# Two copies of the payload and slot buffers, used in turn by the groups of a routed attention and expert kernel

## The chip, the cores and the metric

The kernel runs on one core of a Trainium2 chip. The metric is the device time of the launch in microseconds, as the median of several runs. TensorE (PE), VectorE (DVE), ScalarE (ACT), GpSimd (POOL) and SyncE (SP) each run their own queue of instructions and meet at semaphores. DMAs are issued by SP, ACT and POOL and carried out by 16 DMA engines.

## What is computed

The input `x` is 16 x 128 x 256 (2048 tokens of width 256). First comes a gated convolutional attention, then a layer norm and a routed mixture of experts, both added to `x` (cut from the reference):

```python
kv = jnp.einsum('bhil,bhjl->bijhl', k_, v_)                     # k = v = ctx
y = irfft(rfft(kv, n=512) * rfft(ssm_kernel, n=512))[..., :256] # causal convolution
out = jnp.einsum('bijhl,bhil->bjhl', y + kv * D, q_)            # q = layernorm(x)
x = x + tanh(g_xattn) * out
# experts: E=32 of width 176, the best 6 by score, from 4 of 8 groups, and a shared one
scores = sigmoid(xf @ w_router); sfc = scores + corr_bias       # xf = layernorm(x)
topk_idx = top_k(where(group_mask, sfc, -inf), 6)
routed = sum over the 6 of scores[e] * (silu(xf @ gate_w[e]) * (xf @ up_w[e])) @ down_w[e]
shared = silu(xf @ sh_gate_w) * (xf @ sh_up_w) @ sh_down_w
x = x + tanh(g_ffn) * (routed + shared)
```

## The kernel before

The work has three stages.

**Stage one: the groups.** The 16 batch rows are taken in NG = 4 groups of GB = 4, so 512 tokens in each. A step `group(g, attend, route)` exists on each compute engine. It routes group g and, beside it, does the attention of group g + 1; the first step (g = -1) only attends, the last one (g = 3) only routes. The order within a step is written out by hand on each engine:

- VectorE: products of the context for the next group (L574), then the attention's result is added to `rows` (L715), a layer norm (L551 to L565, which ends by raising `norm_done`), the first half of the product with q and the sum of pairs of the next group (`times_q(0)`, L590, and `sum_pairs(0)`, L603), then `choose()` (from L620: it picks six experts per token) and `place_rows` (L695 to L704: it writes the place of each token in its experts' lists into `slots`), and then the second half of the next group. In group 3 there is no next group, so `choose()` follows the norm at once.
- ScalarE: normalizes and copies; before the rows of group g are written into `payload` (L448) it waits at L444 for `norm_done` and at L445 for `payload_free`.
- TensorE: attention transposes (L909), convolution (L898, L899), transposes of `payload` (L921), router (L965), shared expert (L930, L940, L949).
- POOL: for each group it waits for `slots_ready`, then issues 24 indirect DMAs (L358), each of which scatters 128 rows of 289 floats (256 of the row, the token's number, 32 scores) from `payload` to the experts' lists in HBM, waits until all 24 have landed (L361) and raises `payload_free` (L362). It is raised once before the groups.
- SP: for each group it stores four tiles of the shared expert's result to HBM (`store_shared`, L255 to L261), one after another: each is waited for before the next is issued. ScalarE's copy of a tile to be stored (L419) waits for its buffer, one of two.

**The expert weights** fill one SBUF arena, `w_gu` (32 experts, one row of each of the 128 partitions for all) and `w_down` behind it (88 partitions). The same arena holds what the groups work on, so only a part of the weights can be loaded early: experts 0 to EARLY - 1 of `w_gu` (L253, by SP at the start). The rest of `w_gu` and the first WD_MID experts of `w_down` are loaded by ScalarE in the last group, right behind the writing of `payload` (L454 to L457); the next ones up to WD_LAST by ScalarE when the tables are ready (L483), the last ones by SP behind its last store (L267).

**Stage two: the loop over expert tiles.** SP waits for the tables and for `payload_free` of all groups (L283, L284), reads some values from a table, and loads the first tiles of 128 rows from the lists to `payload` (L274). TensorE waits for all weights and then does, per tile, transposes (L1018), gate and up (L1027), transposes (L1037) and down (L1046). POOL adds each result to the tokens' sums in HBM (L372). There are 108 tiles.

**Stage three**: the sums are loaded, added to `rows` (L871 to L875) and stored.

Of the kernel before, what the change touches and what calls it, by code (L numbers as in the profile page):

```python
# [5 lines left out]
P = 128  # L6
B, HD, L = 16, 128, 256
NH, DH = 16, 8
BLK = L // P
GB = 4  # L10
# [15 lines left out]
TOK_AT, SCORE_AT = L, L + 1  # L26
EARLY = 15
EPS = 1e-5
# [18 lines left out]
WIDE_AT = TMP_AT + TMP_SIZE - 3 * P  # L47
X2T_AT = TMP_AT + TMP_SIZE
SILU_AT = X2T_AT + GB * L
# [32 lines left out]
def build(nc, x, ctx_t, toeplitz, g_xattn, g_ffn, skip_d, w_router, corr_bias,  # L82
# [10 lines left out]
    with ctx:  # L93
# [34 lines left out]
        earlier = sb("earlier", [P, NGRP, NGRP])  # L128
        slots = sb("slots", [P, GB, DH], u32)
        norm_x = sb("norm_x", [P, 2, B])  # L130
# [12 lines left out]
        ctx_v = win(arena, CTX_AT, [[BLK * HD * GB, NG], [HD * GB, BLK], [DH * GB, NH], [1, DH * GB]])  # L143
        toe_v = win(arena, TOE_AT, [[L, NH], [1, L]])
        router_sb = win(arena, ROUTER_AT, [[E, KC], [1, E]])
        stats = win(arena, STATS_AT, [[6, B], [1, 6]])
# [82 lines left out]
        def _(sp):  # L229
# [35 lines left out]
            store_shared(NG - 1)  # L265

            sp.dma_start(wd[:, WD_LAST * WD_E:E * WD_E], w_down[:, WD_LAST * WD_E:E * WD_E]).then_inc(late_in, 16)  # L267

# [34 lines left out]
        def _(pool):  # L303
# [49 lines left out]
            for g in range(NG):  # L353
                pool.wait_ge(slots_ready, g + 1)
                pool.sem_inc(held, 1)
                for b in range(GB):
                    for k in range(TOPK):
                        nc.gpsimd.indirect_dma_start(  # L358
                            lists, bass.IndirectOffsetOnAxis(ap=slots[:, b, k:k + 1], axis=0),
                            payload[:, b, :], None).then_inc(scattered, 16)  # L360
                pool.wait_ge(scattered, (g + 1) * (GB * TOPK * 16))  # L361
                pool.sem_inc(payload_free, 1)  # L362
# [30 lines left out]
        def _(act):  # L393
# [4 lines left out]
            def group(g, attend, route):  # L398
# [43 lines left out]
                if route:  # L442

                    act.wait_ge(norm_done, g + 1)  # L444
                    act.wait_ge(payload_free, g + 1)  # L445
                    act.sem_inc(held, 1)
                    for b in range(GB):
                        last = nc.scalar.activation(payload[:, b, 0:L], rows[:, bass.ds(g * GB + b, 1), :],  # L448
                                                    ACT.Identity, bias=norm[:, 1, b:b + 1], scale=norm[:, 0, b:b + 1])
# [8 lines left out]
                    for p in range(2):  # L458
# [4 lines left out]
                    act.wait_ge(logits_ready, g + 1)  # L463
                    nc.scalar.activation(payload[:, :, SCORE_AT:ROW], win(bank[4], 0, [[E, GB], [1, E]]),
                                         ACT.Sigmoid).then_inc(scores_ready, 1)
# [11 lines left out]
            for g in range(NG - 1):  # L477
# [3 lines left out]

            act.wait_ge(tables_ready, 1)
            act.dma_start(wd[:, WD_MID * WD_E:WD_LAST * WD_E],  # L483
                          w_down[:, WD_MID * WD_E:WD_LAST * WD_E]).then_inc(late_in, 16)
# [47 lines left out]
        def _(dve):  # L532
            count = [0]

            def group(g, attend, route, start):
# [81 lines left out]
                def choose():  # L617

                    dve.wait_ge(scores_ready, g + 1)
                    nc.vector.tensor_copy(payload[:, :, TOK_AT], tok_id[:, bass.ds(g * GB, GB)])  # L620
                    at = [TMP_AT]
# [10 lines left out]

                    scores = payload[:, :, SCORE_AT:ROW]
                    sfc = tmp(GB, E)
# [55 lines left out]
                def place_rows(onehot, part, bke, tmp):  # L690
# [12 lines left out]
                                                 AX, ALU.add))  # L703
                    nc.vector.tensor_copy(slots[:, :, 0:TOPK], win(arena, slot_f, [[TOPK, GB], [1, TOPK]])).then_inc(slots_ready, 1)  # L704

# [174 lines left out]
        def _(pe):  # L880
# [6 lines left out]
            def group(g, attend, route):  # L887
# [71 lines left out]
                if route:  # L959
                    transpose_rows(lambda b, k: payload[:, b, k * P:(k + 1) * P],  # L960
                                   x2_ready, lambda p: g * 2 + p + 1, 0, x2T_ready)
# [155 lines left out]
```

## Time and profile before

| | |
|---|---|
| median of 3 runs | 627.01 us |
| lowest, highest | 623.39, 627.03 us |
| the profiled execution | 621.08 us (span of the instructions 619.0 us) |
| mean granted TensorE clock in it | 0.886 |
| busy in it: PE, DVE, ACT, POOL | 469.5, 331.4, 204.0, 281.4 us |

The rows come from the one profiled execution. Times are from the start of the span. An idle wait is put down to the instruction that ended it ("releaser"); `x24` is the number of instructions in a row of a view. A letter q behind an engine's name (ACTq, POOLq, SPq) marks its queue's own instructions: DMA issues, semaphores, register loads. The DMA queues are q0 (issued by POOL), q1 (by SP) and q10 (by ACT).

### The profile page before, as it was taken

How to read it: one execution, taken by the hardware profiler on the slowest of the kernel's cores; microseconds unless marked ns; L12 is line 12 of the kernel's file. 1: busy time of each engine (PE TensorE's matmuls, PEld its weight loads, DVE VectorE, ACT ScalarE, POOL GpSimd, SP SyncE). 2: the span in 40 equal slices, each digit the busy share in tenths (PEclk: the TensorE clock that was granted, in tenths of full speed). 3: DMA queues.
4: the chain of work that ended last, by engine and by line, in shares of the span. 5: the costliest groups of instructions: out<-in, count | busy, mean ns of one | idle time of the engine just before them, and what ended most of it. 6: DMA issues, size and time to landing. Idle time of an engine off the chain costs nothing.

```text
span 619.0 us, 8968 instructions
## 1 busy us (share of the span) xinstructions
PE 469.5 (76%) x2271; PEld 358.6 (58%) x2271; DVE 331.4 (54%) x1169; ACT 204.0 (33%) x510; POOL 281.4 (45%) x243
## 2 busy tenths in 40 slices
PE   0365889959968981692069999999999999999900
PEld 0355766846756671471047777777777777777600
DVE  3798689578866931660024444444444444444327
ACT  2140632443335312220014444444444444444400
POOL 3600006711770374067106666666666666666620
PEclk9996989959996996686569999999999999999955
DMA  7999103300330134977636666666666666666478
GB/s 266 346 342 434 56 1 112 125 29 16 134 116 0 53 136 176 356 183 221 164 79 108 115 111 115 112 116 118 110 110 114 119 111 113 111 116 120 64 232 337
DMA packets 55756, 89.70 MB, mean 145 GB/s; under 512 B 6573, under 2 KB 49933, under 8 KB 55053
## 3 DMA queue, kind: packets, MB, share of 16 engines
q0 software_dynamic: 20160, 28.37, 26.5%
q1 hardware_dynamic: 35198, 49.87, 24.3%
q10 hardware_dynamic: 342, 10.81, 5.7%
q8 instruction: 24, 0.39, 0.3%
q14 instruction: 32, 0.25, 0.1%
HBM read 47.00 MB, written 42.03 MB: 144 GB/s over the span
## 4 chain that ended last, share of the span: by engine, by line
PE 51%; POOL 13%; DMA 13%; DVE 13%; issue 6%; ACT 2%; SPq 1%; POOLq 0%; DVEq 0%; ACTq 0%
PE bank L1027 21%; PE bank L1046 15%; POOL expert_lists L358 12%; DMA token_sums<-arena 6%; PE bank L1018 4%; PE bank L1037 4%; DVE arena L590 3%; DMA arena<-token_sums 2%; DMA arena<-toeplitz 2%; PE bank L965 2%; DVE work L603 2%; PE bank L909 2%; PE bank L921 1%; DMA expert_lists<-payload,slots 1%; PE bank L898 1%
## 5 line engine op out<-in xcount | busy, mean ns | idle before, releaser
L372 POOL DMA_INDIRECT token_sums<-work,dest x108 | 168.3, 1558 | 127.1 <-ACT work L505 103.5
L358 POOL DMA_INDIRECT expert_lists<-payload,slots x96 | 98.8, 1029 | 172.3 <-DVE slots L704 144.2
L1027 PE MATMUL bank<-wgu,work 128*128 x432 | 148.1, 466 | 0.1
L1046 PE MATMUL bank<-wd,work 88*128 x432 | 111.0, 379 | 0.0
L849 DVE TENSOR_TENSOR work<-work,bank 128x176 f32<-128x176 f32 x108 | 36.4, 337 | 121.7 <-ACT work L490 121.7
L1027 PEld LDWEIGHTS bank<-wgu,work 128*128 128x128 f32 x432 | 74.5, 192 | 24.0 <-issue 1.5
L831 DVE COPY work<-bank 128x256 f32<-128x256 f32 x108 | 45.8, 424 | 60.0 <-PE bank L1018 60.0
L1046 PEld LDWEIGHTS bank<-wd,work 88*128 88x128 f32 x432 | 73.3, 190 | 6.1 <-issue 0.2
L490 ACT ACTIVATE work<-bank 128x176 f32<-128x176 f32 x108 | 34.2, 317 | 126.6 <-PE bank L1027 126.6
L505 ACT ACTIVATE work<-bank,work 128x256 f32<-128x256 f32 x108 | 51.1, 473 | 53.6 <-DVE work L843 52.3
L1018 PE MATMUL bank<-ident,payload 128*128 128x128 f32 x216 | 42.1, 276 | 23.5 <-DMA payload<-expert_lists 23.5
L1018 PEld LDWEIGHTS bank<-ident,payload 128*128 128x128 f32 x216 | 30.8, 144 | 35.4 <-DMA payload<-expert_lists 24.2
L930 PE MATMUL bank<-shgu_sb,arena 128*128 128x352 f32 x128 | 51.3, 554 | 0.0
L590 DVE TENSOR_TENSOR arena<-arena,q_sb 128x448 f32<-128x448 f32 (+7 forms) x120 | 43.2, 434 | 7.9 <-ACT arena L405 7.8
L898 PE MATMUL bank<-arena 128*128 128x288 f32 x128 | 43.9, 426 | 1.2 <-ACT arena L405 1.2
L1037 PEld LDWEIGHTS bank<-ident,work 128*88 128x88 f32 x216 | 26.6, 123 | 30.3 <-issue 19.0
L1037 PE MATMUL bank<-ident,work 128*88 128x128 f32 x216 | 41.3, 273 | 0.0
L949 PE MATMUL bank<-shd_sb,arena 88*128 88x256 f32 x128 | 32.9, 402 | 11.1 <-ACT arena L414 10.1
L909 PE MATMUL bank<-ident,work 128*128 128x128 f32 x256 | 31.3, 286 | 12.9 <-DVE work L603 12.9
L497 ACT COPY work<-bank 88x256 f32<-88x256 f32 x108 | 39.7, 367 | 0.0
L909 PEld LDWEIGHTS bank<-ident,work 128*128 128x128 f32 x256 | 31.2, 203 | 13.2 <-issue 13.1
L930 PEld LDWEIGHTS bank<-shgu_sb,arena 128*128 128x128 f32 x128 | 28.5, 234 | 14.3 <-issue 7.2
(140 smaller groups left out, 512.1 us busy)
## 6 DMA issues: line engine op xcount, KB each, us to landing
payload<-expert_lists SPq DMA_DIRECT2D x108, 144.5 KB, 2.6
arena<-token_sums SPq DMA_DIRECT2D x12, 512.0 KB, 8.3
wgu<-w_gu ACTq DMA_DIRECT2D x1, 5984.0 KB
wgu<-w_gu SPq DMA_DIRECT2D x1, 5280.0 KB, 31.3
expert_lists<-blank SPq DMA_DIRECT2D x1, 4768.5 KB, 24.2
token_sums<-blank SPq DMA_DIRECT2D x1, 4480.0 KB, 34.3
wd<-w_down ACTq DMA_DIRECT2D x1, 3520.0 KB
arena<-toeplitz SPq DMA_DIRECT2D x1, 2048.0 KB, 11.3
```

What stands on the lines that cost most here:

```text
L358: nc.gpsimd.indirect_dma_start(lists, bass.IndirectOffsetOnAxis(ap=slots[:, b, k:k + 1], axis=0), payload[:, b, :], None).then_inc(scatter ...
L372: nc.gpsimd.indirect_dma_start(sums, bass.IndirectOffsetOnAxis(ap=dest[:, t % NPICK:t % NPICK + 1], axis=0), y_row(t), None, compute_op=AL ...
L505: nc.scalar.activation(y_row(t), bank[6 + t % 2][:, 0:L], ACT.Identity, scale=pick_w(t)).then_inc(t_y_copied, 1)
L590: last = nc.vector.tensor_tensor(win(arena, Z_AT + z0, [[DH * DH * GB, HB], [(DH + 1) * GB, DH - d], [1, GB]]), y, win(q_sb, s * HB * DH * ...
L831: nc.vector.tensor_copy(win(work, XT_AT + t % 2 * L, [[1, L]]), bank[t % 2][:, 0:L]).then_inc(t_x, 1)
L898: nc.tensor.matmul(y[:, 0:2 * CB], toe(h, 0), prods(s, hh, 0, 2), start=True, stop=False)
L909: last = nc.tensor.matmul(bank[p][:, (b * BLK + k) * P:(b * BLK + k + 1) * P], win(work, ((k * 4 + i) * GB + 2 * p + b) * P, [[1, P]]), id ...
L930: last = nc.tensor.matmul(bank[5 + half][:, 0:SHM], x2T(b, k), shgu_sb[:, k, half * SHM:(half + 1) * SHM], start=(k == 0), stop=(k == KC - 1))
L1018: last = nc.tensor.transpose(bank[t % 2][:, k * P:(k + 1) * P], payload[:, t % NX, k * P:(k + 1) * P], ident[:, :])
L1027: last = nc.tensor.matmul(bank[2 + t % 2][:, 0:2 * M], xT_half(t, k), wgu[:, bass.ds(e * WGU_E + k * 2 * M, 2 * M)], start=(k == 0), stop= ...
L1037: last = nc.tensor.transpose(bank[4 + t % 2][0:MH, c * P:(c + 1) * P], win(work, H_AT + t % 2 * M + c * MH, [[1, MH]]), ident[:, :])
L1046: last = nc.tensor.matmul(bank[6 + t % 2][:, 0:L], hT_half(t, c), wd[:, bass.ds(e * WD_E + c * L, L)], start=(c == 0), stop=(c == 1))
```

## The change

Two copies of `payload` are used in turn: groups 0 and 2 write a new one, `pay[0]`, which lies in the arena, groups 1 and 3 the old one. `slots` gets a second copy as well. ScalarE waits before it writes group g's rows for the scatters of group g - 2, no longer for those of group g - 1. Since the arena has to hold 1156 floats per partition more, what lies in front of it moves down by two experts' `w_gu`: EARLY is 13 for 15, so 19 experts of `w_gu` are loaded late for 17 (6688 KB for 5984), with WD_MID = 17 and WD_LAST = 25 for 20 and 26. The first late part of `w_down` is so 17 experts for 20, the second 8 for 6, the last 7 for 6. The second and the last part would overwrite `pay[0]`, so they wait for group 2's scatters.

```diff
-EARLY = 15
+EARLY = 13
...
-X2T_AT = TMP_AT + TMP_SIZE
+PAY_AT = TMP_AT + TMP_SIZE
+X2T_AT = PAY_AT + GB * ROW
...
-        slots = sb("slots", [P, GB, DH], u32)
+        slots = sb("slots", [P, 2, GB, DH], u32)
...
+        pay = [win(arena, PAY_AT, [[ROW, GB], [1, ROW]]), payload[:, :, :]]
...
+            sp.wait_ge(payload_free, NG)
             sp.dma_start(wd[:, WD_LAST * WD_E:E * WD_E], w_down[:, WD_LAST * WD_E:E * WD_E]).then_inc(late_in, 16)
...
-                            lists, bass.IndirectOffsetOnAxis(ap=slots[:, b, k:k + 1], axis=0),
-                            payload[:, b, :], None).then_inc(scattered, 16)
+                            lists, bass.IndirectOffsetOnAxis(ap=slots[:, g % 2, b, k:k + 1], axis=0),
+                            pay[g % 2][:, b, :], None).then_inc(scattered, 16)
...
-                    act.wait_ge(payload_free, g + 1)
+                    act.wait_ge(payload_free, max(1, g))
                     act.sem_inc(held, 1)
                     for b in range(GB):
-                        last = nc.scalar.activation(payload[:, b, 0:L], rows[:, bass.ds(g * GB + b, 1), :],
+                        last = nc.scalar.activation(pay[g % 2][:, b, 0:L], rows[:, bass.ds(g * GB + b, 1), :],
...
-                    nc.scalar.activation(payload[:, :, SCORE_AT:ROW], win(bank[4], 0, [[E, GB], [1, E]]),
+                    nc.scalar.activation(pay[g % 2][:, :, SCORE_AT:ROW], win(bank[4], 0, [[E, GB], [1, E]]),
...
             act.wait_ge(tables_ready, 1)
+            act.wait_ge(payload_free, NG)
             act.dma_start(wd[:, WD_MID * WD_E:WD_LAST * WD_E],
...
-                    nc.vector.tensor_copy(payload[:, :, TOK_AT], tok_id[:, bass.ds(g * GB, GB)])
+                    nc.vector.tensor_copy(pay[g % 2][:, :, TOK_AT], tok_id[:, bass.ds(g * GB, GB)])
...
-                    scores = payload[:, :, SCORE_AT:ROW]
+                    scores = pay[g % 2][:, :, SCORE_AT:ROW]
...
-                    nc.vector.tensor_copy(slots[:, :, 0:TOPK], win(arena, slot_f, [[TOPK, GB], [1, TOPK]])).then_inc(slots_ready, 1)
+                    nc.vector.tensor_copy(slots[:, g % 2, :, 0:TOPK], win(arena, slot_f, [[TOPK, GB], [1, TOPK]])).then_inc(slots_ready, 1)
...
-                    transpose_rows(lambda b, k: payload[:, b, k * P:(k + 1) * P],
+                    transpose_rows(lambda b, k: pay[g % 2][:, b, k * P:(k + 1) * P],
```

## Rows read from the trace of the kernel before

**Rows 1.** The page's chain that ended last, by line, as shares of the span.
```profile
PE bank L1027 21%; PE bank L1046 15%; POOL expert_lists L358 12%; DMA token_sums<-arena 6%; PE bank L1018 4%; PE bank L1037 4%; DVE arena L590 3%; DMA arena<-token_sums 2%; DMA arena<-toeplitz 2%; PE bank L965 2%; DVE work L603 2%; PE bank L909 2%; PE bank L921 1%; DMA expert_lists<-payload,slots 1%; PE bank L898 1%
```

**Rows 2.** By stretch: busy us of PE, PEld, DVE, ACT, POOL; clock, DMA share, GB/s.
```profile
350.00:588.00 238.00, 236.93 (x1142) 175.52 (x1140) 107.55 (x470) 101.92 (x288) 149.61 (x97) 1.00 0.66 111
```

**Rows 3.** Waits: who waited for whom, us in total, times, longest us.
```profile
ACT payload L448 <- POOLq L362: 30.9, 3, 19.5
```

**Rows 4.** Timeline of DVE, groups 1 and 2: start, us, instructions, [idle before, releaser].
```profile
129.15 3.77 DVE L603 TENSOR_TENSOR work<-arena 128x256 f32<-128x256 f32 x8
137.25 0.17 DVE L620 COPY payload<-tok_id 128x4 f32<-128x4 f32 x1 [4.33 <-ACT payload L464]
...
186.22 3.77 DVE L603 TENSOR_TENSOR work<-arena 128x256 f32<-128x256 f32 x8
194.54 0.17 DVE L620 COPY payload<-tok_id 128x4 f32<-128x4 f32 x1 [4.56 <-ACT payload L464]
```

**Rows 5.** Timelines of DVE and ACT in group 3.
```profile
235.37 0.16 DVE L565 SCALAR_TENSOR_TENSOR norm<-arena,norm 128x4 f32<-128x4 f32 x1
...
242.90 0.60 ACT L448 ACTIVATE payload<-rows,norm 128x256 f32<-128x256 f32 x1 [19.45 <-POOLq L362]
243.01 0.38 ACTq L455 DMA_DIRECT2D wgu<-w_gu  x1
...
250.79 0.17 DVE L620 COPY payload<-tok_id 128x4 f32<-128x4 f32 x1 [15.26 <-ACT payload L464]
```

**Rows 6.** POOL: last scatter of group 2, first and last of group 3; L362's first and last.
```profile
240.00 0.96 POOL L358 DMA_INDIRECT expert_lists<-payload,slots  x1 [0.30 <-issue]
265.99 0.96 POOL L358 DMA_INDIRECT expert_lists<-payload,slots  x1 [25.03 <-DVE slots L704]
...
295.14 0.96 POOL L358 DMA_INDIRECT expert_lists<-payload,slots  x1 [0.30 <-issue]
...
L362 POOLq EVENT_SEMAPHORE  x4: 17/17/17, 129.2 to 302.4; - x4
```

**Rows 7.** DMA queues (packets, MB, share) in 209-243, 244-259, 260-265, 270-275, 265-280, 283-284 us.
```profile
q0 software_dynamic: 1152, 3.55, 28.9%
...
q10 hardware_dynamic: 142, 6.33, 103.6%
...
q10 hardware_dynamic: 20, 0.82, 79.8%
...
q1 hardware_dynamic: 45, 0.04, 2.3%
...
q10 hardware_dynamic: 47, 1.93, 56.9%
q0 software_dynamic: 176, 0.56, 11.3%
q1 hardware_dynamic: 61, 0.06, 1.4%
...
q10 hardware_dynamic: 8, 0.00, 0.7%
```

**Rows 8.** Chain that ended last, in order of time: start, us, what.
```profile
269.14 16.85 DMA token_sums<-arena
...
286.07 6.24 DMA token_sums<-arena
...
292.38 9.54 DMA token_sums<-arena
...
303.80 0.34 SPq L267
...
305.51 7.86 DMA payload<-expert_lists
...
314.21 1.19 PE bank L1018 x4
```

**Rows 9.** The page's DMA issues: tiles, queue, count, KB each, median us to landing.
```profile
payload<-expert_lists SPq DMA_DIRECT2D x108, 144.5 KB, 2.6
```

## The prediction

> **What bounds the kernel now.** I read the page's chain by line first [rows 1]: 44% of the span is TensorE in the loop over expert tiles (L1027, L1046, L1018, L1037), and 12% is POOL at L358, the scatters of routed rows. The table by stretches [rows 2] shows that loop full: from 350 to 588 us TensorE is busy 236.93 of 238 us at full clock. The change leaves that loop and the tail alone (108 tiles, same instructions), so what it is worth is how much earlier the loop's first transpose (314.21 us, [rows 8]) comes.
>
> In the first part the wait to look for is ScalarE's at L448, for the queue of POOL at L362 [rows 3]: 30.9 us in three waits, the longest 19.5. A group may not write `payload` before the scatters of the group before have landed. TensorE and VectorE stand behind it.
>
> After the last group two lines of work run to the loop's start [rows 6, 8]. One is POOL: 24 scatters from 265.99, the last issued at 295.14, all landed at 302.4 [rows 6]. The other is SP: four stores of the shared expert's rows, one after another (16.85, 6.24, 9.54 us and a short one), then the last part of `w_down` at 303.80 and the first tile's load at 305.51. They end 1.4 us apart. Both are slow for one reason, the late expert weights issued at 243.01.
>
> **The change, part by part.**
>
> *Group 1.* Its L448 starts at 129.28, when payload comes free, 5.58 us late. VectorE gives part of that back: it sums pairs from 129.15 for 3.77 us (to 132.92) and only then starts to choose experts, at 137.25 [rows 4]. Without the wait the scores, which let 137.25 go, come 5.6 us earlier (131.6), before 132.92. So choosing starts at 132.95: 4.3 us gained, not 5.6.
>
> *Group 2.* The same: 186.22 + 3.77 = 189.99, against 194.54 [rows 4]: 4.5 us. Together 8.8.
>
> *Group 3.* There is no next group's attention to do. The norm's last step is issued at 235.37 for 0.16 us and L448 starts at 242.90 [rows 5]. Allowing 0.2 us it would start at 235.7: 7.2 us. Nothing else of VectorE's lies between, so this shows in full: choosing at 250.79 − 16.0 = 234.8, and slots for the last scatters 16.0 us earlier too; POOL could start them at 265.99 − 16.0 = 250.0.
>
> The new waits for scatters two groups back cost nothing here: group 2 needs those of group 0 (landed 129.2, [rows 6]) at some 176, group 3 those of group 1 (landed some 57 us later, a group's period, less 4) at 227. The copies' other address, and `slots` with one more dimension, add no instruction.
>
> *What comes next.* If everything followed, the loop would start 16 us earlier. But the wait also held back the late weights. ScalarE issues them right behind L448: 243.01 becomes 227.0, with the first bytes about 1 us later, at 227.9. POOL issues one scatter each 29.15/23 = 1.27 us, group 2's last at 240.00 [rows 6], after the change 231.2. It lands about 2.8 us from the start of its issue (240.00, and L448 goes on at 242.90). So the last five, issued from 226.1 on, have packets left when the weights begin. Before, all had landed first.
>
> What that costs is read from group 3's scatters, which run beside the weights' second part. One scatter is 1152/24 = 48 packets [rows 7], 3 per DMA engine. Of the weights' 142 packets from 244 to 259 us some 133 carry data (6.33 MB of 48 KB each, `w_gu`'s rows), which makes 1.036 × 15 us × 16/133 = 1.87 us for one on its engine; a `w_down` packet is 41 KB and took 0.798 × 5 × 16/20 = 3.2 us, before any scatter ran beside it [rows 7]. `w_gu`'s 128 rows are 8 packets per engine and are through at about 259.2. `w_down` has 88 rows. Of the first shared store's 144 packets (9 per engine) 45 went through in 270 to 275 us, at once, and only 16 more by 280: so 5 engines are free and 11 work on `w_down`, 8 packets each [rows 7, 8]. From 265 to 280 us 176 scatter packets went through; ten scatters had reached the free engines, 5 × 3 × 10 = 150; the other 26 passed on the 11 busy ones beside 47 weight packets, 0.55 small ones to a large one. The small packets wait behind large ones, and few pass.
>
> After the change five scatters leave 15 small packets per engine, with 8 + 8 = 16 large ones on the 11 busy engines. At 0.55 per large one some 9 pass before the weights end, and the shared store's went at a similar pace (16 packets on 11 engines in 5 us), so the scatters land when the weights end. The end: before, first bytes 243.9, `w_gu` to 259.2, the last data at 283.6 (from 283 to 284 its queue shows only packets without data, [rows 7]). After, 19 experts for 17 make `w_gu` 15.2 × 19/17 = 17.0 us, 17 for 20 make `w_down` 24.4 × 17/20 = 20.7 us, and the extra small packets cost 1.3 us (ten data packets of 0.2 us, less what the 24.4 hold already): 227.9 + 39.0 = 266.9. POOL waits for them before it may start group 3's, which I put 0.8 us later: **267.8**. Before it was 265.99. The 16 us that the groups give are gone for POOL.
>
> If instead one small packet passed for each large one, the 15th small one would be through before the last large one starts, 20.7/8 = 2.6 us before the weights' end: POOL starts at 265.0. The row's 0.55 is below that. The Trainium skill, "DMA: Bandwidth & Descriptors", section "Queues, rings and completion order", says that each DMA engine takes the queues in turn, a packet from each; by that rule the alternation is strict and the loop starts 13 us earlier, by the row 10.
>
> *From there to the loop.* Last scatter 29.15 us after the first (265.99 to 295.14), landing 2.75 us as group 2's last one did (group 3's own took 7.3, [rows 6], beside the second part of `w_down`, which now comes 20 us earlier), SP's value loads 1.4 us (303.80 to 305.51 less 0.34 of issue), the first load 2.6 us (the median, [rows 9]; here 7.86 behind the last part of `w_down`), and 0.1 to 0.84 us until TensorE starts (take 0.2): 267.8 + 29.15 + 2.75 + 1.4 + 2.6 + 0.2 = 303.9, against 314.21: **10.3 us**.
>
> *The stores, against it.* The first lands 2.4 us behind the weights' end (285.99 against 283.6, [rows 8]), 269.3; the second has no backlog of group 3's scatters beside it (some 2 us, not 6.24), 271.3; the third lies beside the second part of `w_down`, now 8 experts for 6: 9.54 × 8/6 = 12.7 at most, 284; the fourth 1.7; the last part of `w_down`, 7 for 6, some 8 to 10 us: 296. That is 8 us ahead of 303.9. The costs of the shift in weights (704 KB more late `w_gu`, 528 KB less late `w_down` of the first part) are in the sum above, the early load of 13 for 15 experts lies beside group 0's attention and nothing waits for it until the loop.
>
> **The rivals.**
>
> *Scatters pass freely.* If group 2's five scatters land in time for slots (250.0), POOL is done at 282, and the stores decide: first at 269.3, second 6.2 beside group 3's backlog, third 9.5 to 12.7, fourth 1.7, then 10.4 to 11.6 from the last part of `w_down` to TensorE: 298 to 302, 12 to 16 us gained. For it: the five free engines pass all. Against it: a DMA is done when all 16 are.
>
> *Strict alternation* (above, one small packet to a large one): POOL starts at 265.0, 13.1 us gained. Against it the 0.55; for it, that the 0.55 comes from a time with two small queues.
>
> *A longer stall.* The backlog of 15 packets per engine isn't drained when weights end, or the shared stores take turns too: each 1 us is 1 us. At 5 us more, 5 us gained.
>
> *Slower than before.* `w_gu` packets now share the engines with scatters. If that brought them to the `w_down` packets' rate (41 KB in 3.2 us, so 53.5 KB in 4.2), 8 of them take 33.6 us for 17: POOL starts at 284.4, 6 us slower than before. It decides from 3.4 us a packet, at which the 10.3 us are gone. Against it: `w_down` packets were that slow with no scatter about.
>
> *It doesn't do what it says*: L448 still waits for the old scatters. Nothing in the diff does that.
>
> **How the numbers follow.** The profiled execution took 621.08 us (span 619.0); less 10.3 it is 610.8. The median of the three runs is 627.01, 6 us above it, and 623.39 the lowest; I forecast against the median: 616.7. Chances: landing at the weights' end 0.50, strict alternation 0.17, scatters pass freely 0.15, a longer stall 0.12, slower 0.03, no effect 0.03. The range from 16 us gained (611), less 2 for a median as near to the profiled run as 623.39 is, to 5 gained (622): 609 to 622. About 1% (6.3 us) is what a measurement tells from no change. Faster by over 1%: 0.86; within: 0.10; slower: 0.04.
>
> **What would show it.** L448 no longer waits for L362; choosing starts at 133.0, 185.7 and 234.8; weights issued at 227; group 2's last scatter lands at 264 to 269 and POOL starts group 3's right behind it, at 268, some 18 us after its slots are ready; SP waits at L284 for payload_free from about 296; the loop starts at 304. I am wrong if POOL starts at 250, if ScalarE finds group 1's scatters not landed, or if the loop's start moves and the end doesn't.

## The result, and the profile after

| | before | after |
|---|---|---|
| median | 625.96 us of 4 runs (623.39 to 627.03) | 608.29 us of 4 runs (607.58 to 608.84) |
| ratio, 95% interval | | 0.972 (0.969 to 0.976) |
| the profiled execution | 621.08 us (span 619.0) | 607.58 us (span 605.5) |
| mean granted TensorE clock | 0.886 | 0.894 |
| first transpose of the loop | 314.21 us | 301.71 us |

The change gains 17.7 us in the medians and 13.5 us between the two profiled executions. The forecast was 616.7 us with 609 as its lower end, so it came out too slow by 8.4 us, and just outside its range. Line numbers from L358 on are three or four higher after the change (L448 is L451, L358 is L361, L620 is L624).

VectorE's timeline after the change, at the lines where choosing starts (start, us, what, in brackets the idle time before and its releaser). The tile named `arena` is the new copy of the payload.

```profile
131.89 0.17 DVE L624 COPY payload<-tok_id 128x4 f32<-128x4 f32 x1
...
186.15 0.17 DVE L624 COPY arena<-tok_id 128x4 f32<-128x4 f32 x1
...
236.64 0.17 DVE L624 COPY payload<-tok_id 128x4 f32<-128x4 f32 x1 [8.04 <-ACT payload L467]
...
250.83 0.18 DVE L708 CAST slots<-arena 128x24 uint32<-128x24 f32 x1
```

Before, these three stood at 137.25, 194.54 and 250.79 [rows 4, 5]. The groups give 14.15 us by the last one; 16.0 was forecast. ScalarE's timeline in the last group shows the wait for POOL gone and the late weights issued right behind the first row of the payload:

```profile
228.74 0.60 ACT L451 ACTIVATE payload<-rows,norm 128x256 f32<-128x256 f32 x1 [12.06 <-DVE norm L569]
228.85 0.38 ACTq L458 DMA_DIRECT2D wgu<-w_gu  x1
```

POOL's timeline: the last scatter of group 2, then the first and the last of group 3; the last line is POOL's signal that a group's scatters have landed, with its first and last start.

```profile
231.11 0.96 POOL L361 DMA_INDIRECT expert_lists<-arena,slots  x1 [0.30 <-issue]
252.21 0.95 POOL L361 DMA_INDIRECT expert_lists<-payload,slots  x1 [20.14 <-DMA expert_lists<-arena,slots]
...
281.26 0.96 POOL L361 DMA_INDIRECT expert_lists<-payload,slots  x1 [0.30 <-issue]
...
L365 POOLq EVENT_SEMAPHORE  x4: 17/17/17, 128.3 to 289.9; - x4
```

And the chain that ended last, in order of time (start, us, what). It runs through the four stores of the shared expert's rows, the last part of `w_down` and the first tile's load:

```profile
254.72 15.87 DMA token_sums<-arena
270.67 6.25 DMA token_sums<-arena
277.00 11.61 DMA token_sums<-arena
288.69 1.74 DMA token_sums<-arena
290.51 0.34 SPq L270
292.22 8.82 DMA payload<-expert_lists
301.71 0.70 PE bank L1022 x2
```

The last scatter of group 2 was issued at 231.11, its last packet left an engine at 250.4, and it landed at 251.3 (20.2 us after its issue), where 266.9 was forecast. That is 0.3 us behind the slots (250.83 + 0.18). Before, POOL started 1.00 us after the writing of the slots began (264.99 and 265.99), here 1.38 us after, so some 0.4 us of its wait is still for the scatters. The stores decided the loop's start, with POOL's last landing (289.9) 0.6 us ahead of them.

### The profile page after: what moved, and what is told of

Read it like the earlier page. It is cut to its first block, busy times and chain, and to the rows that moved or that the text cites. A ratio compares the mean times of both kernels' runs of the same rounds, so it can differ in the third digit from the quotient of the medians.

```text
span 605.5 us, 8969 instructions
## 1 busy us (share of the span) xinstructions
PE 468.5 (77%) x2271; PEld 358.6 (59%) x2271; DVE 330.8 (55%) x1169; ACT 203.6 (34%) x510; POOL 281.0 (46%) x243
## 4 chain that ended last, share of the span: by engine, by line
PE 62%; DVE 18%; DMA 12%; ACT 2%; issue 2%; POOL 2%; SPq 1%; DVEq 0%; POOLq 0%; ACTq 0%
PE bank L1031 21%; PE bank L1050 15%; DMA token_sums<-arena 6%; DVE arena L594 6%; PE bank L913 5%; PE bank L1022 4%; PE bank L1041 4%; PE bank L934 4%; PE bank L953 3%; DVE work L607 3%; PE bank L902 2%; DMA arena<-toeplitz 2%; DMA arena<-token_sums 2%; DMA payload<-expert_lists 1%; DMA token_sums<-work,dest 1%
## 5 line engine op out<-in xcount | busy, mean ns | idle before, releaser
L361 POOL DMA_INDIRECT expert_lists<-arena,slots x48 | 49.6, 1033 | 105.1 <-DVE slots L708 91.1
L361 POOL DMA_INDIRECT expert_lists<-payload,slots x48 | 48.9, 1020 | 54.6 <-DVE slots L708 20.4
L934 PE MATMUL bank<-shgu_sb,arena 128*128 128x352 f32 x128 | 52.8, 567 | 0.0
L902 PE MATMUL bank<-arena 128*128 128x288 f32 x128 | 43.9, 426 | 1.2 <-ACT arena L408 1.2
L953 PE MATMUL bank<-shd_sb,arena 88*128 88x256 f32 x128 | 32.6, 400 | 9.5 <-ACT arena L417 9.2
```

The lines of the kernel that those rows point to most:

```text
L361: nc.gpsimd.indirect_dma_start(lists, bass.IndirectOffsetOnAxis(ap=slots[:, g % 2, b, k:k + 1], axis=0), pay[g % 2][:, b, :], None).then_i ...
L902: nc.tensor.matmul(y[:, 0:2 * CB], toe(h, 0), prods(s, hh, 0, 2), start=True, stop=False)
L934: last = nc.tensor.matmul(bank[5 + half][:, 0:SHM], x2T(b, k), shgu_sb[:, k, half * SHM:(half + 1) * SHM], start=(k == 0), stop=(k == KC - 1))
L953: last = nc.tensor.matmul(bank[4][:, 0:L], win(arena, HST_AT + c * P, [[1, P]], parts=MH), shd_sb[:, c, :], start=(c == 0), stop=(c == 3))
```

## Experiments

The theory at this point: the last group's stores decide, and group 2's scatters pass the weights because few of them are left when the weights begin. Rivals: the layout itself (fewer early experts) gives or costs something; the wait in the last group matters, or only those in groups 1 and 2; the part of the gain that the traces don't show is chance. The runs were made on several chips. Each has its own runs of the kernel before beside it.

### Taking the change apart, on a chip where it brings nothing

The edits are against the changed kernel (one line replaces another, three variants shown together). The first keeps the layout and both copies but waits as the old kernel does; the second takes the gain in groups 1 and 2 alone; the third in group 3 alone; the fourth is the changed kernel unedited.

```diff
-                    act.wait_ge(payload_free, max(1, g))
+                    act.wait_ge(payload_free, g + 1)                                       # layout only
+                    act.wait_ge(payload_free, g + 1 if g == NG - 1 else max(1, g))         # groups 1 and 2
+                    act.wait_ge(payload_free, g if g == NG - 1 else g + 1)                 # group 3
```

> The changed kernel with ScalarE's old wait put back (for the scatters of the group before): two copies, EARLY 13 and the new split of the late weights stay. Theory (the gain is the wait, the layout is neutral): the loop starts within 2 us of before's 314.2, time within 2 us of before. Rival (part of the 13 us of the traces comes from the layout, since less w_down and more w_gu goes into the first late part): 3 us or more faster than before, loop start at 311 or earlier.

> The changed kernel, but in the last group ScalarE waits for group 2's scatters as before; groups 1 and 2 don't. Theory (the loop starts a fixed stretch after the late weights are issued, because the shared stores stand behind them): weights issued at about 234 (scatters of group 2 landed), 9 us earlier than before and 5 later than in the changed kernel; loop start at 306 to 307, 7 to 8 us faster than before. Rival (the five scatters beside the weights cost the changed kernel something): as fast as the changed kernel or faster.

> The changed kernel, but groups 1 and 2 wait as before and only the last group does not. Theory: choosing starts at 137 and 194.5 as before, the last group's L448 follows the norm at about 236, 7 us earlier than before, so the weights are issued 7 us earlier and the loop starts 5 to 7 us earlier; together with the run of groups 1 and 2 the gains add up to the whole. Rival (POOL, not the stores, decides): group 2's scatters land only when the weights end, POOL starts the last group's no earlier than before (266) and the gain is under 2 us.

> The changed kernel again, on the chip of the three others. Theory (its runs agree and those of the kernel before spread by some us, the profiled one of before being the lowest): 607 to 609 us in each run, the kernel before at 621 to 627. Rival (the chip of the first comparison was odd): the kernel before within 1 us of 621, gain of 13 us as in the traces.

Measured, against a before of 659.9 us (31 runs): layout only 1.002 (0.999 to 1.005), groups 1 and 2 1.006 (1.001 to 1.010), group 3 1.002 (0.998 to 1.006), the changed kernel 1.006 (1.002 to 1.010). On this chip the kernel before takes 34 us more than on the first and the changed one 55 us more, and the change was worth nothing; if anything it cost 0.6%. No theory expected this. Waits of the changed kernel on this chip (who waited for whom, us in total, times, longest us), and two gaps in the timeline of weight loads to TensorE:

```profile
PEld bank L902 <- issue: 14.1, 8, 3.6
PEld bank L953 <- issue: 12.3, 9, 4.9
...
121.98 0.30 PEld L902 LDWEIGHTS bank<-arena 128*128 128x128 f32 x2 [2.44 <-issue]
126.27 0.50 PEld L902 LDWEIGHTS bank<-arena 128*128 128x128 f32 x2 [3.44 <-issue]
```

TensorE's stream of instructions stands still for microseconds while scatters run, with nothing in the profile that it waits for. The same waits on the first chip are 0.4 us (L902) and 0.2 us (L953) in all. TensorE isn't alone: in the same trace VectorE stands for 2.82 us before L719 and ScalarE for 4.62 us before L408, also with no releaser. Choosing here starts at 80.19, 146.55 and 213.18 us: a group takes 66 us instead of 53 to 54. Scatters then have landed long before the next payload is written. In the layout-only kernel, which still waits for them, the wait is not there to remove; ScalarE's one long wait at that line is for the norm:

```profile
ACT payload L451 <- DVE norm L569: 25.6, 1, 25.6
```

So on a chip in this condition the wait for `payload_free` costs nothing, and taking it away gives nothing. Why the engines stand still there was not found.

### The stores taken away, on a second such chip

The last group's four tiles go to four places in `q_sb`, free by then, so that ScalarE needn't wait for a buffer nor SP for a store.

```diff
-            store_shared(NG - 1)
+            for b in range(GB):
+                sp.wait_ge(sh_copied, (NG - 1) * GB + b + 1)
+                sp.dma_start(sums[0:T, :]..., win(q_sb, b * L, [[L, 1], [1, L]])).then_inc(sh_stored, 16)
...
-                    act.wait_ge(shared_free, g * GB + b + 1)
+                    if attend:
+                        act.wait_ge(shared_free, g * GB + b + 1)
...
+                    nc.scalar.copy(... if attend else win(q_sb, b * L, [[1, L]]), bank[4][:, 0:L])...
```

> The changed kernel, and in the last group the four tiles of the shared expert's result go to four buffers (q_sb, which that group has no use for) and are stored without a wait between them; the last part of w_down then follows their issue. In a loop start decided by the stores (first store's 15.9 us, then 6.3, 11.6 and 1.7, last part of w_down at 290.5): stores issued by 262, second and last part of w_down issued by 263, loop start 5 to 10 us earlier than the changed kernel's 301.7, then bound by POOL's scatters (last issued at 281, landed by 285 to 290). Rival (POOL's scatters decide already): loop start within 2 us of the changed kernel's.

Measured: 657.69 against 656.08 us, ratio 1.001 (0.997 to 1.006). The chip was again one where TensorE stands still, so this says nothing of the stores on the others. It was run again below.

### The weights in small packets

The two late loads behind the payload are cut into eight, so that a packet is 8 to 14 KB for 52 (`w_gu`) and 34 (`w_down`). TensorE's wait for the weights counts the added loads (not in the excerpt).

```diff
-                        act.dma_start(wgu[:, EARLY * WGU_E:E * WGU_E], ...).then_inc(late_in, 16)
-                        act.dma_start(wd[:, 0:WD_MID * WD_E], ...).then_inc(late_in, 16)
+                        for i, j in ((13, 18), (18, 23), (23, 28), (28, 32)):
+                            act.dma_start(wgu[:, i * WGU_E:j * WGU_E], ...).then_inc(late_in, 16)
+                        for i, j in ((0, 5), (5, 9), (9, 13), (13, 17)):
+                            act.dma_start(wd[:, i * WD_E:j * WD_E], ...).then_inc(late_in, 16)
```

> The changed kernel with the two late loads that ScalarE issues in the last group cut into eight (w_gu in parts of 5, 5, 5 and 4 experts, w_down in 5, 4, 4 and 4), so that a packet is 8 to 14 KB and not 35 to 54. Theory (each DMA engine takes a packet from each queue in turn, so a small packet waits for one large one): group 2's scatters and the first shared store get through three to four times faster; the first store lands in 3 to 6 us, not 15.9, though the weights end at about the same time. Rival (the store waits for the bytes of the weights, whatever their packets): it still takes 13 us or more.

Measured: a single run of each, 605.2 us against 623.67 us for the kernel before, so this is no comparison of medians. POOL's start no longer waits for any DMA, but for its slots:

```profile
255.74 0.96 POOL L361 DMA_INDIRECT expert_lists<-payload,slots  x1 [22.14 <-DVE slots L709]
...
284.89 3.18 DMA expert_lists<-payload,slots
289.47 8.68 DMA payload<-expert_lists
```

The scatters passed the weights. POOL started 3.5 us later than in the changed kernel: the weights were issued 2.1 us later in this execution (230.94), and eight issues on ScalarE delayed the scores by some 2 us more. The first store took 9.9 us, between the 3 to 6 of the theory and the 13 of its rival: it landed when the weights ended, at 268. From the first store's issue to the last one's landing it was some 29 us, where the changed kernel took 35.7. SP then still had to wait 0.5 us for POOL. The loop started at 298.87, for 301.71.

### The parts again, on a chip that behaves as the first

> The changed kernel with ScalarE's old wait put back, again, on another chip, since on the first TensorE stood still for microseconds beside the scatters. Theory (the gain is the wait, the layout is neutral): the loop starts within 2 us of before's 314.2 and the time is within 3 us of before's. Rival (part of the gain is the layout): 4 us or more faster than before.

> The wait relaxed in groups 1 and 2 only, again, on another chip. Theory (the loop starts a fixed stretch, some 73 us, after the late weights are issued): weights issued at about 234 and loop start at 306 to 307, 7 to 9 us faster than before, 5 slower than the changed kernel. Rival (group 2's scatters beside the weights cost the changed kernel something): within 2 us of the changed kernel.

> The wait relaxed in the last group only, again, on another chip. Theory: weights issued at about 236, loop start at 307 to 309, 5 to 7 us faster than before. Rival (POOL decides and its last 24 scatters start no earlier than before's 266, as the prediction had it): under 2 us.

| kernel | median | against before (625.0, 19 runs) | weights issued | loop starts |
|---|---|---|---|---|
| layout only | 625.5 | 1.000 (0.998 to 1.001) | 246.82 | 319.35 |
| groups 1 and 2 | 613.44 | 0.983 (0.978 to 0.987) | 235.12 | 306.99 |
| group 3 | 621.74 | 0.995 (0.993 to 0.997) | 237.72 | 312.67 |

The layout costs nothing. Groups 1 and 2 are worth 12 us, more than the 8.8 that the forecast gave them, and group 3 alone is worth 3.8 us, less than the theory's 5 to 7. Why groups 1 and 2 give more than forecast shows on ScalarE (the waits for the old scatters), first in the profile of before:

```profile
129.28 2.08 ACT L448 ACTIVATE payload<-rows,norm 128x256 f32<-128x256 f32 x4 [5.58 <-POOLq L362]
186.57 2.08 ACT L448 ACTIVATE payload<-rows,norm 128x256 f32<-128x256 f32 x4 [5.87 <-POOLq L362]
```

In the layout-only kernel, with one scatter each of groups 0 and 1 on POOL:

```profile
130.87 2.08 ACT L451 ACTIVATE payload<-rows,norm 128x256 f32<-128x256 f32 x4 [6.80 <-POOLq L365]
190.36 2.08 ACT L451 ACTIVATE arena<-rows,norm 128x256 f32<-128x256 f32 x4 [8.05 <-POOLq L365]
...
108.52 3.59 POOL L361 DMA_INDIRECT expert_lists<-arena,slots  x1 [0.30 <-issue]
166.78 3.59 POOL L361 DMA_INDIRECT expert_lists<-payload,slots  x1 [0.30 <-issue]
```

Most scatters are issued in 0.96 us and some in 3.59; the profile of before has none above 1.58. In a kernel that waits for them, each such one delays the next group. The kernel with group 3 alone bears it out: it waits 5.32 us in group 1, with no long scatter ahead, and 7.99 us in group 2, with one (at 165.17). Less the 1.3 us that VectorE gives back in each group, 6.80 and 8.05 make 12.3 us, and the weights came 11.7 us earlier. That the two agree so well is partly chance: the two executions start to choose 1.2 us apart, and TensorE ran slow in one group of the one and in two of the other (see below). In the changed kernel nobody waits. That would fit the spread too, 623.39 to 627.03 us before and 607.58 to 608.84 after, but no trace of a slower run of before is there to show it.

Group 3 alone is the forecast's mechanism in full, and the rival of this run came true in it: POOL decided. Four scatters of group 2 were behind the weights. The chain, and POOL's timeline:

```profile
241.61 26.58 DMA expert_lists<-arena,slots
...
269.09 0.95 POOL L361 DMA_INDIRECT expert_lists<-payload,slots  x1 [26.53 <-DMA expert_lists<-arena,slots]
...
298.17 10.86 DMA expert_lists<-payload,slots
```

POOL started 31.4 us after the weights' issue and decided the loop's start. In the changed kernel it started 23.4 us after, with three scatters behind the weights. Queues over the stretch from the weights' first bytes to the landing (packets, MB, share of 16 engines), first of the changed kernel (229.8 to 251.5 us), then of group 3 alone (238.7 to 268.5):

```profile
q10 hardware_dynamic: 166, 7.61, 90.9%
q0 software_dynamic: 144, 0.44, 5.1%
```

```profile
q10 hardware_dynamic: 199, 8.76, 84.1%
q0 software_dynamic: 192, 0.59, 5.8%
q1 hardware_dynamic: 45, 0.04, 0.4%
```

144 packets are 3 scatters, 9 packets per engine; 192 are 4 scatters, 12 per engine. Of q10's, 128 are `w_gu`'s (53.5 KB each, with KB of 1000 bytes here, 6.85 MB) and the rest of the bytes make 22 `w_down` packets of 34.8 KB in the first case and 55 in the second, which on 11 engines is 2 and 5 each (16 more carry no data): 8 + 2 = 10 large ones beside 9 small ones, and 8 + 5 = 13 beside 12. That is one small packet to one large one, behind one large one of head start. The fourth scatter's three packets per engine wait for three packets of `w_down`, and these are what the 8 us between 23.4 and 31.4 pay for, an estimate of 2.7 us each.

### The stores taken away, again

The same edit as on the second chip.

> The changed kernel with the last group's four shared stores in buffers of their own and without waits between them, again, on another chip. Theory (in the changed kernel the stores decide the loop's start): all weights are issued by 264, the loop starts at 290 to 296, 6 to 11 us earlier than in the changed kernel, bound then by POOL's scatters. Rival (the weights' bytes decide in any order): within 3 us of the changed kernel.

Measured: 606.79 us, ratio 0.970 (0.966 to 0.974); the changed kernel in the first batch, on another chip, had 0.972. Expected was a loop start at 290 to 296, it came at 300.15, within 3 us of the changed kernel's, as the rival had it. The chain:

```profile
282.85 13.68 DMA expert_lists<-payload,slots
298.76 2.33 DMA payload<-expert_lists
```

POOL had started and ended its issues within 1.6 us of the changed kernel's. The landing took 13.68 us, 5 more than there, because without the stores' waits both remaining parts of `w_down` are issued at 268.0 and 268.72 and are moved beside the scatters. In the changed kernel the stores were last, but right behind them comes POOL. Whether the bytes of the weights would hold the loop up in any order, as the rival says, this run doesn't settle. Here too three scatters were issued late enough to be caught, and POOL started 23.5 us after the weights' issue.

### TensorE kept busy ahead of the shared expert

In the changed kernel TensorE idles 2.6 to 3.1 us for VectorE before the shared expert's products of each attending group. TensorE's timeline, and a table of 6 us (busy us and instructions of PE, PEld, DVE, ACT, POOL; granted clock, DMA share, GB/s):

```profile
196.57 0.81 PE L944 MATMUL bank<-ident,arena 128*88 128x128 f32 x4 [2.86 <-DVE arena L618]
197.38 4.04 PE L934 MATMUL bank<-shgu_sb,arena 128*128 128x352 f32 x8
...
196.00:202.00 6.00, 5.43 (x18) 3.77 (x19) 3.01 (x8) 1.04 (x2) 0.92 (x1) 0.72 0.00 0
```

The kernel before, at the same place of the same group:

```profile
205.01 0.64 PE L940 MATMUL bank<-ident,arena 128*88 128x128 f32 x4 [0.57 <-DVE arena L614]
205.60 2.59 PE L930 MATMUL bank<-shgu_sb,arena 128*128 128x352 f32 x8
...
205.00:211.00 6.00, 5.69 (x27) 4.16 (x28) 4.74 (x10) 1.46 (x4) 1.45 (x2) 1.00 0.00 0
```

The same eight products take 4.04 us for 2.59 (3.73 us in group 1, behind 3.07 us idle). In group 0, before and after the change, TensorE idled 2.59 us at this place and the products still took 2.59. Of 6 us the granted clock is 0.72 on average, which is some 3.4 us at 1.2 GHz and the rest at 2.4. This could be the 1.5 us per group that the forecast missed. The edit adds four matrix products whose result nobody reads:

```diff
+                    if attend:
+                        for _ in range(4):
+                            nc.tensor.matmul(bank[7][:, :], ident[:, :], shgu_sb[:, 0, 0:512], start=True, stop=True)
```

> The changed kernel with four extra matmuls of 512 columns (their result is not used) on TensorE before L944 in the groups that also attend, where the changed kernel lets it idle 3.6 us before it works at half clock (L934 3.5 to 3.8 us for 8, before 2.6). Theory (each group lost 1.5 us of its gain to that clock): L934 back at 2.6 us, choosing of groups 2 and 3 1.5 and 3 us earlier, time 1 to 3 us shorter. Rival (the 1.5 us per group come from VectorE's own work, e.g. the pause of 0.4 us in the pair sums): no gain, or slower by the matmuls' time.

Measured: 608.28 us, ratio 0.974 (0.970 to 0.978) against its own before of 624.64. The time did not fall by the 1 to 3 us expected. The products and then POOL:

```profile
197.91 2.58 PE L934 MATMUL bank<-shgu_sb,arena 128*128 128x352 f32 x8
...
259.57 0.96 POOL L361 DMA_INDIRECT expert_lists<-payload,slots  x1 [26.27 <-DMA expert_lists<-arena,slots]
```

The clock is 1.00 in this stretch and in that of group 1 (140 to 148 us, 0.79 in the changed kernel). From group 1's choosing to group 2's it takes 52.72 us for 54.26, as the forecast had it (52.7), and from there to group 3's 49.48 for 50.49. From group 0's to group 1's, where the changed kernel had run at full clock, the added products cost 0.5 us (53.20 for 52.70). The weights are issued at 228.13, 0.7 us earlier than in the changed kernel, while group 2's last scatter is issued 1.24 us later (232.35), since POOL started later and several of its issues were longer. Together that puts a fourth scatter behind the weights: POOL starts 7.4 us later, and the loop at 302.51 us against 301.71. So the clock's cost in the groups is shown, some 2.5 us in all; that it is given back at the weights is only in part due to their coming earlier.

### The weights ahead of the scatters' end, in small packets

With the stores' edit, SP issues the late weights as soon as the arena is free, at 220 us, in nine parts. ScalarE's two loads are taken out, and TensorE's wait counts the new ones (neither is in the excerpt).

```diff
+            sp.wait_ge(pairs_summed, 2 * NG)
+            for i, j in ((13, 17), (17, 21), (21, 25), (25, 29), (29, 32)):
+                sp.dma_start(wgu[:, i * WGU_E:j * WGU_E], ...).then_inc(late_in, 16)
+            for i, j in ((0, 5), (5, 9), (9, 13), (13, 17)):
+                sp.dma_start(wd[:, i * WD_E:j * WD_E], ...).then_inc(late_in, 16)
```

> The changed kernel with the last group's shared stores in own buffers and no waits between them, and the late weights issued by SP as soon as the last pair sum is done (about 217), in nine parts. Theory (packets of the scatters wait one large packet each, so small large ones let group 2's scatters land in time, and nothing then stands before POOL's last 24): weights issued 11 us earlier, POOL starts the last group's at 252, all landed by 285 to 288, loop start at 288 to 293, time 596 to 601. Rival (more scatters stand behind the weights, 12 of 24, and land later than the slots are ready): POOL starts at 255 or later and the gain over the changed kernel is under 3 us.

Measured: 601.84 us (601.15 to 602.46), ratio 0.963 (0.960 to 0.967): 6.4 us better than the four products beside it. POOL waits for its slots alone, and the landing of the last group is 9.55 us:

```profile
253.33 0.96 POOL L369 DMA_INDIRECT expert_lists<-payload,slots  x1 [20.33 <-DVE slots L712]
...
282.62 9.55 DMA expert_lists<-payload,slots
294.38 2.33 DMA payload<-expert_lists
```

The loop starts at 295.75, 6 us earlier than in the changed kernel. The theory had asked for more: time 596 to 601, loop at 288 to 293, and the last landing by 288, where it came at 292.2, beside the last parts of `w_down` (issued at 269.05 and 269.75). But the rival (POOL at 255 or later, under 3 us gained) is out. Three things were changed at once here (stores, time of issue, packets), and this run doesn't tell their shares apart. The queues from 228 to 240 us show that small weight packets and scatter packets pass about one to one as well:

```profile
q1 hardware_dynamic: 394, 3.83, 76.0%
q0 software_dynamic: 387, 1.20, 25.3%
```

This is the fastest version found, and beats both kernels.

## Why the forecast was wrong, point by point

**Right: what bounds, and what the change frees.** L451 no longer waits for POOL, and group 3 finds its buffer free. VectorE's sums of pairs do take back part of the gain in groups 1 and 2.

**Groups: 16.0 us forecast, 14.15 measured.** The missing 1.85 us is two losses of 1.5 us less a head start. From group 1's choosing to group 2's it took 54.26 us where 52.7 was forecast, from there to group 3's 50.49 for 49.1. In both, the shared expert's products ran slow (granted clock 0.79 and 0.72) behind a 3 us wait, where TensorE had waited 0.93 and 0.57 us before; with TensorE kept busy these stretches took 52.72 and 49.48. Against them stands that the first choosing came at 79.19 for 80.24, before any wait was removed. It lay between 78.7 and 80.5 in the profiles of the other kernels, so that part looks like chance. The forecast moved VectorE's work earlier and left TensorE's durations as they were.

**The step that failed: five scatters behind the weights.** The forecast had the weights at 227.0 and took every scatter issued from 226.1 on as caught, that is, with packets still to move when the weights' packets arrive. Group 2's last was issued at 231.11, forecast 231.2. The weights' first bytes came at 229.86, and three scatters, those issued at 228.58, 229.84 and 231.11, were caught; the one of 227.31 was not.

With four caught in the two other kernels, where the weights came 1.6 us sooner against the scatters, the border lies between 1.3 us ahead of the first bytes (the scatter of 228.58) and 2.1 us (in the kernel with TensorE kept busy, the scatter of 227.29 was not caught by first bytes at 229.42). The forecast took the 2.8 us from issue to landing for it. But in the profile of before the packets of the last scatter, issued at 240.00, passed between 241.5 and 242.1 us, and only its landing came at 242.8. The first of the forecast's five was issued 1.8 us ahead of 227.9, which is within that border, so by this alone four or five would have been caught; the rest is that the weights came 1.9 us later, which is one and a half scatters.

So 9 packets per engine waited, not 15. The last was through at 250.4 and its landing came at 251.3, 0.3 us behind the slots, not at 266.9. The mechanism itself is real and about as costly as forecast: with four scatters caught POOL starts 31.4 us after the weights' issue (both kernels where it happened, 269.09 - 237.72 and 259.57 - 228.13), which is some 8 us more than the 23.4 and 23.5 with three. It is a matter of counts: a shift of one scatter, 1.27 us, decides 8 us.

**The rate of 0.55 was mis-sized too.** With one small queue beside the weights the counts come to 1 to 1. The 0.55 was read where q0 and q1 both had small packets [rows 7]. With q1's 61 - 45 = 16 on the 11 busy engines added to POOL's 26 it is 42 small ones beside 47 large ones, 0.9. So the two small queues appear to share one turn between them against the large one; that is argued from the counts of one trace, and no run was made to test it. The Trainium skill, "DMA: Bandwidth & Descriptors", section "Queues, rings and completion order", says that a DMA engine takes its queues in turn, a packet from each. The counts with one small queue agree (9 small to 10 large, 12 to 13). For two small queues they agree less well. By 1 to 1 and one large packet of head start, five scatters would have waited for the 16 large packets of the weights, so until their end or, as the forecast's own rival had it, 2.8 us less. The rate alone would not have mended the forecast; the count did the harm.

**The rival that came true: scatters pass freely.** It gave 298 to 302 us for the loop's start, decided by the stores; it was 301.71. It had 0.15, since the forecast argued that a DMA is done only when all 16 engines are, and then took the count for given. The argument held: in the kernel with group 3 alone the fourth scatter landed at 268.2, when the engines with `w_down` packets had moved its share, though five engines had no such packets. The rival's own reason, that the five free engines pass all, is not what happened: three scatters were caught, and they landed in time for the slots to within 0.4 us. So its number came true without its mechanism. Of its terms the second store measured 6.25 (6.2), the third 11.61 (9.5 to 12.7), the end from the last part of `w_down` to TensorE 11.2 (10.4 to 11.6).

**Landing of the last group: 2.75 us forecast, 8.6 measured** (281.26 to 289.9). The forecast had the second part of `w_down` come 20 us earlier and be out of the way. It came 15 us earlier, at 277.0 for 292.4, since ScalarE issues it behind the last copies for the shared stores, which wait for their buffers. So POOL's landing took 6 us longer than forecast, and the stores' chain was 6 us longer as well (290.51 for the last part where 286 was forecast, then 11.2 for 10). Where POOL did start as late as forecast, in the kernel with group 3 alone, the loop came 43.6 us behind its start (312.67 - 269.09) for 36.1 forecast: this term again.

**The base.** The forecast took its 10.3 us from the median, 627.01, though the terms were read from a profiled execution of 621.08. The changed kernel's runs lie within 1.3 us, the old one's within 3.6, and the profiled execution of before was faster than all four of them. The waits that are removed vary with the scatters: 5.3 to 5.9 us where none is long, 6.8 to 8.05 where one is. So the profiled execution probably shows less of that wait than the median has: 17.7 us gained in medians, 13.5 between the traces. That this is the whole of the 4.2 us is not shown. 12.5 of the 13.5 lie before the loop and 1.0 in it; the loop and tail of all kernels here took 303.7 to 305.6 us.

**Adding up the 8.4 us**: the loop started 12.5 us earlier instead of 10.3 (2.2); the loop and tail 1.0; the gap between the profiled execution and the median 4.2 more; the first median against the one of this comparison (627.01 and 625.96) 1.0.

## What to carry to other kernels

When a removed wait also held back a large transfer, count which small transfers are still in flight at its first byte, in packets per engine, and ask what one unit more or less of them does: here one scatter more costs 8 us, so the range belongs around that count. When the wait removed is a wait for something whose duration varies, its price in one profiled execution is one draw; price it against several runs. And when two chains end 1 us apart, taking away the one that is last shows the other: size both to the end.

## What the runs showed of the hardware

- A queue of 35 to 54 KB packets and one of small packets take turns on a DMA engine, by counts of 10 large to 9 small and 13 to 12. So each packet that a scatter still has there waits for one of those, an estimate of 2.7 us for a `w_down` packet. Cut to 8 to 14 KB, the weights let the scatters land before the slots were ready.
- TensorE, idle for 2.86 to 3.07 us, then ran the same products in 3.73 to 4.04 us for 2.59, at a granted clock of 0.79 and 0.72 on average over the 8 and 6 us around them. With four products more ahead of them (the experiment above) the clock stayed at 1.00. An idle 2.59 us was followed by full speed in the profiles of before and after (group 0), and one of 2.61 us by 4.28 us for the products in two others (layout only, stores free). So nearly the same idle time doesn't always end the same way. With the stores free, the clock was still 1.00 while TensorE idled (87.9 to 90.5 us) and 0.50 from 92 to 94 us.
- Some scatters take 3.59 us of POOL for 0.96, and a kernel that waits for the group's scatters waits 1 to 3 us longer then (6.80 to 8.05 for 5.32 to 5.87). What marks them was not found.
- On two of the chips the engines stood still during the scatters with nothing to wait for in the profile, TensorE most, for 1 to 5 us at a time and once for 9.0, but ScalarE and VectorE too. Kernels there took 656 to 664 us, and neither the change nor the stores' edit moved them by more than 0.6%. The cause is open.
